# Attention with keys and values made beside it: the product with the values moved between two pieces of keys and values

## The reference

```python
q = (x @ Wq + bq).reshape(B, N, H, hd).transpose(0, 2, 1, 3)
kv = (ctx @ Wkv + bkv).reshape(B, K, 2, H, hd).transpose(2, 0, 3, 1, 4)
k, v = (kv[0], kv[1])
attn = jnp.einsum('bhnd,bhkd->bhnk', q * SCALE, k)
attn = jax.nn.softmax(attn, axis=-1)
out = jnp.einsum('bhnk,bhkd->bhnd', attn, v)
```

## Time and profile before

| | |
|---|---|
| median of 3 runs | 1428.68 us (1428.05 to 1432.59) |
| the profiled execution | 1433.56 us, its span 1431.5 us |
| PE busy | 1331.0 us, 93% |
| DVE, ACT, GpSimd busy | 937.2, 759.0, 101.6 us |
| DMA | 146.15 MB, mean 102 GB/s |
| mean granted TensorE clock | 0.974 |
| the batch loop (seven passes) | 81.80 to 880.86 us of the span |

### The profile page before, as it was taken

How to read it: one execution, slowest core, us unless ns; L and a number is a source line. 1 busy time by engine, 2 the same in 40 slices (tenths; PEclk the granted TensorE clock), 3 DMA queues, 4 the chain that set the end, 5 groups by cost and what they waited for, 6 DMA issues and landing times.

```text
span 1431.5 us, 21997 instructions
## 1 busy us (share of the span) xinstructions
PE 1331.0 (93%) x7407; PEld 1151.9 (80%) x7408; DVE 937.2 (65%) x1498; ACT 759.0 (53%) x1320; POOL 101.6 (7%) x75
## 2 busy tenths in 40 slices
PE   5999999999999999999999999956898799999995
PEld 4888888899889889888898889845777577878774
DVE  3666666667567666666666666648489836578772
ACT  3455565566556555555555555533332526578770
POOL 0000000000000000000000000063243120000001
PEclk9999999999999999999999999977899899999997
DMA  5121011110101112112101110570548357399983
GB/s 191 55 71 49 27 44 44 33 44 22 52 19 50 29 33 59 29 29 60 33 26 44 44 33 16 105 176 16 106 122 305 130 198 257 133 338 343 341 284 96
DMA packets 129443, 146.15 MB, mean 102 GB/s; under 512 B 66408, under 2 KB 69864, under 8 KB 129392
## 3 DMA queue, kind: packets, MB, share of 16 engines
q1 hardware_dynamic: 128128, 141.49, 32.1%
q0 software_dynamic: 1280, 4.20, 0.9%
HBM read 125.02 MB, written 20.12 MB: 101 GB/s over the span
## 4 chain that ended last, share of the span: by engine, by line
PE 70%; DVE 14%; issue 6%; DMA 5%; ACT 4%; SPq 1%; DVEq 0%; POOL 0%; ACTq 0%; POOLq 0%
PE ps_scores L151 12%; PE ps_scores L153 12%; PE ps_scores L152 12%; PE ps_out L779 6%; PE ps_turn L767 5%; PE ps_scores L756 5%; PE ps_turn L665 2%; DVE stat L621 2%; PE ps_scores L2009 2%; PE ps_scores L2007 2%; PE ps_scores L2008 2%; DMA wu_raw<-in_L_ffn_W_dram 2%; DMA b1rows<-b_parts 2%; DVE Ks L531 2%; DVE wu_lo L1903 1%
## 5 line engine op out<-in xcount | busy, mean ns | idle before, releaser
L531 DVE SCALAR_TENSOR_TENSOR Ks<-ps_scores,bkc,Ks 64x384 fp32r<-64x384 f32 (+2 forms) x254 | 160.5, 632 | 147.9 <-ACT Ks L415 144.8
L151 PE MATMUL ps_scores<-cT_hi,Wkv_hi 128*128 128x384 f32 (+2 forms) x508 | 184.6, 363 | 6.4 <-DVE Wkv_lo L553 6.4
L493 ACT ACTIVATE Pr<-ps_scores,stat 128x705 f32<-128x705 f32 (+1 forms) x128 | 119.6, 934 | 115.5 <-DVE stat L621 115.5
L153 PE MATMUL ps_scores<-cT_hi,Wkv_lo 128*128 128x384 f32 (+2 forms) x508 | 175.4, 345 | 0.0
L152 PE MATMUL ps_scores<-cT_lo,Wkv_hi 128*128 128x384 f32 (+2 forms) x508 | 175.0, 344 | 0.0
L415 ACT ACTIVATE Ks<-ps_scores,bkc 64x384 fp32r<-64x384 f32 (+2 forms) x254 | 149.6, 589 | 43.0 <-PE ps_scores L153 41.2
L151 PE MATMUL ps_scores<-Wkv_hi,cT_hi 128*128 128x512 f32 (+1 forms) x412 | 170.6, 414 | 0.5 <-DVE Ks L531 0.5
L480 ACT CAST PT<-ps_turn 128x512 fp32r<-128x512 f32 (+2 forms) x256 | 110.2, 483 | 110.4 <-PE ps_turn L767 109.6
L537 DVE TENSOR_TENSOR Vs<-ps_scores,Vs 128x512 fp32r<-128x512 f32 (+1 forms) x103 | 71.2, 691 | 148.9 <-ACT Vs L419 148.3
L153 PE MATMUL ps_scores<-Wkv_hi,cT_lo 128*128 128x512 f32 (+1 forms) x412 | 162.4, 394 | 0.0
L152 PE MATMUL ps_scores<-Wkv_lo,cT_hi 128*128 128x512 f32 (+1 forms) x412 | 161.8, 393 | 0.0
(11 more groups left out here) (355 smaller groups left out, 2455.0 us busy)
## 6 DMA issues: line engine op xcount, KB each, us to landing
wu_raw<-in_L_ffn_W_dram SPq DMA_DIRECT2D x64, 1024.0 KB, 7.5
raw<-in_ctx_dram SPq DMA_DIRECT2D x16, 768.0 KB, 4.6
raw<-in_ctx_dram SPq DMA_DIRECT2D x8, 1024.0 KB, 5.3
raw<-in_ctx_dram SPq DMA_DIRECT2D x8, 512.0 KB
sorted_x<-zeros SPq DMA_DIRECT2D x1, 4096.0 KB, 15.1
sorted_out<-zeros SPq DMA_DIRECT2D x1, 4096.0 KB, 25.6
o_heads<-U SPq DMA_DIRECT2D x56, 64.0 KB, 1.7
oA<-o_heads SPq DMA_DIRECT2D x8, 448.0 KB, 9.4
```

What stands on the lines that cost most here:

```text
L151: nc.tensor.matmul(out_ap, sh, mh, start=(i == 0), stop=False)
L153: last = nc.tensor.matmul(out_ap, sl, mh, start=False, stop=(i == len(pairs) - 1))
L493: nc.scalar.activation(Pr[:, i % 2, 0:VALID[c]], S_cols(c, 0, VALID[c]), ACT.Exp, bias=stat[:, 0, c, i:i + 1], accum_out=stat[:, 1, c, i:i ...
L531: ins = nc.vector.scalar_tensor_tensor(out=Ks[c][64:128, j, o:o + wide], in0=acc[64 * h:64 * h + 64, 0:wide], scalar=bkc[:, j:j + 1], in1= ...
```

## The change

In every step that makes pieces, outputs(i) on the tensor engine and the sum into U on the vector engine are issued behind the step's first piece (and the context turn behind it) and ahead of its second piece. Where a step has one piece the order stays what it was, except that work beside the unit now comes behind the outputs on PE in the last batch. In the last unit, which has no pieces, nothing changes. ACT's queue is the same.

```diff
--- before.py
+++ after.py
@@ -615,6 +615,13 @@
                                                           f32(PT[0:TAIL, tiles[-1], 0, :]), ALU.subtract)
                         ins.then_inc(sem("turn_lo"), 1)
 
+                    def sum_outputs(i):
+                        dve.wait_ge(sem("o_made"), pair0 + i)
+                        if i == 1:
+                            dve.wait_ge(sem("u_free"), b * 128 + (128 if beside else 64) * c + 1)
+                        nc.vector.tensor_reduce(U[:, i - 1, :], psO_heads.rearrange("p (a r) -> p r a", a=2),
+                                                AX.X, ALU.add).then_inc(sem("o_summed"), 1)
+
                     for i in range(STEPS):
                         if i < NP:
                             dve.wait_ge(sem("s_made"), pair0 + i + 1)
@@ -629,12 +636,10 @@
                                 if n == first[i] and i < ctx:
                                     cc, s = (1 - c, 1) if i < KC else (c, 0)
                                     ctx_lo(turn0 + turn_of_ctx(i), bank(C_BANK), cc, s, i % KC)
-                        if i >= 1:
-                            dve.wait_ge(sem("o_made"), pair0 + i)
-                            if i == 1:
-                                dve.wait_ge(sem("u_free"), b * 128 + (128 if beside else 64) * c + 1)
-                            nc.vector.tensor_reduce(U[:, i - 1, :], psO_heads.rearrange("p (a r) -> p r a", a=2),
-                                                    AX.X, ALU.add).then_inc(sem("o_summed"), 1)
+                                if n == first[i] and i >= 1:
+                                    sum_outputs(i)
+                        if i >= 1 and not ctx:
+                            sum_outputs(i)
                         if beside:
                             beside(i)
                     if c == 1 and not beside:
@@ -796,9 +801,11 @@
                                 if n == first[i] and i < ctx:
                                     bb, cc, s = (b + c, 1 - c, 1) if i < KC else (b + 1, c, 0)
                                     turn_ctx(turn0 + turn_of_ctx(i), bank(C_BANK), bb, cc, s, i % KC)
+                                if n == first[i] and i >= 1:
+                                    outputs(i)
                         if beside:
                             beside(i)
-                        if i >= 1:
+                        if i >= 1 and not ctx:
                             outputs(i)
 
                 with pe.Fori(0, BE) as b:
```

## The result

The changed kernel takes **1482.07 us** (median of four, 1480.34 to 1483.48) beside 1430.41 of the kernel before: a ratio of 1.0358 [1.0337, 1.0379], 52 us slower (a ratio is given with its 95% interval). Forecast were 1483.1 and a range of 1470 to 1494. The profiled execution took 1483.48, its span 1480.5 against 1431.5.

What follows compares the result with a forecast made beforehand. The tensor engine's in-order queue was taken as the bound. Waits of 3.08 and 3.30 plus 0.7 restart gave 7.1 us per batch, 49.7 for seven; with 4.7 for the last, +54.4: 1483.1 us, range 1470 to 1494.

Steps and rivals of the forecast that it cites:

- the restart: Tensor engine, outputs after a wait: the group spans 0.10 us more for each of seven new waits, 0.7 us per batch.
- The chain and its price: End of piece b to outputs: 4.88 us, without U (0.34) and a context-copy delay (0.23); cover 3.94, so 0.94 us wait.
- step 1: Outputs wait for the probabilities' low parts, per batch: 0.89 us in chunk 0, 0.91 in chunk 1.
- step 2: Outputs behind a step ending with keys wait, per batch: 0.94 us in chunk 0, 0.75 in chunk 1.
- step 5: Outputs wait 0.94 us per batch in each chunk; chunk 0's follows keys 322 wide.
- step 6: One-piece step, its old wait grows: chunk 0 to 0.95 us (+0.31; other count 1.12), chunk 1 to 0.93 (+0.38).
- piece 5: Chunk 1, first piece of step 3: new wait of 0.32 us per batch for the bank of piece 4.
- Steps 3, 4, 7 and 8: Chunk 0, behind values or a single piece whose outputs still follow it: no wait.
- The last pass: Last batch's chunk 0, outside the loop: 4.7 us more together; its chunk 1, without pieces, untouched.
- The faster case: Rival: only the one-piece step's wait changes as U leaves the chain, 8 or 10 us gained, 1420 us; 3 in 100.
- Absorbed in part: Rival: only first-step waits are real, later ones find the vector engine ahead; 16 us more, 1445 us; 5 in 100.
- The clock: Rival: tensor engine idling drops the loop's granted clock to 0.92, costing 69 us more, 1552 us; 2 in 100.

Runs made afterwards that it cites:

- The first run: The changed kernel with the vector engine's sum into U back behind both pieces, only the tensor engine's outputs moved: 1495.3 us, 1.0438 of the kernel before.
- the run with the steps behind values: The kernel before with outputs and sum moved only in steps 4 and 7 of chunk 0 and 3, 4 and 7 of chunk 1: 1436.15 us, 1.0027.
- the late low parts: The changed kernel, vector engine taking most last pieces' low parts behind the next maximum and probabilities' low parts, step 0's context copy behind the maximum: 1423.83 us, 0.9946.

## Why the prediction was right, step by step

- **The number, and the luck in it.** The forecast 1483.1 lies 1.0 from the median, but the growth was forecast as 54.4 and is 51.7; the forecast started from 1428.68, which came out as 1430.41 with a fourth run, and that hides 1.7. In the two profiled spans the growth is 49.0: of the 5.4 that are missing, 4.0 are the loop's (49.7 forecast, 45.7 measured), the restart below, and 1.4 the stretch ahead of the loop.
- **The chain and its price.** Forecast 4.88 us from the end of piece b, measured 4.89. Both things that were to fall out of it did: U stands at 454.11, ahead of the low parts, and those stand behind no context copy. The first run shows U's share by putting it back.
- **The waits, step by step** (forecast, then measured). Chunk 0: step 1 0.89, 0.89; step 2 0.94, 0.96; step 5 0.94, 0.95; step 6 0.95, 0.95. Chunk 1: 0.91, 0.91; 0.75, 0.79; piece 5 0.32, 0.34; 0.94, 0.95; 0.93, 0.95. Steps 3, 4, 7 and 8 wait in neither. For step 6 of chunk 0 two counts stood against each other, 1.12 and 0.94; the second, chain less cover, was right. Taking from and adding to the old wait misses that in the kernel before the low parts stood 0.19 behind a context copy there (462.80 against 462.58 + 0.03), which the later end of piece b takes out. In chunk 1 no copy stood in the way, and the same count gave 0.93 for a measured 0.95. What the new waits add sums to 3.10 + 3.39 = 6.49 a batch, 0.11 above the forecast 6.38 without the restarts.
- **The restart was the term mis-sized**: 0.7 us a batch were forecast, about 0.05 are there (6.54 less 6.49), and this is the forecast's excess of half a microsecond a batch. The outputs do take 0.93 from start to start (451.31 to 452.24) instead of 0.82. But they take as much where they don't wait, as the last section shows, and the piece that now follows them instead of a context turn is shorter by nearly the same: 452.24 to 454.35 is 2.11, where 432.30 to 434.47 was 2.17; 322 wide it is 1.78 for 1.86, 512 wide 2.75 for 2.84. The step that failed is the reading of a longer group behind a wait as the price of the wait, from the two groups that waited, without a look at one behind a context turn that didn't.
- **The two halves of a rule.** The Trainium skill (TensorE: Matmul & The Clock Gate, "Part 2: What happens when you issue a matmul") says that weight loads are pulled ahead of matmuls in flight and that matmuls keep their order. From the first half the prediction drew a rival, a restart that costs nothing. It nearly is so, but not by weights that were loaded ahead over the wait: the loads waited with their products (PEld rows for L609 and L613, 52.5 us in all). The second half the trace shows at each wait: piece b starts at 460.18, behind the outputs of 459.24.
- **The last pass.** Forecast +4.7; from its first scores to the end of the program 4.7 were measured, 4.5 of them in chunk 0's unit itself (54.25 to 58.78). Step 1 waits 1.38 (1.32 forecast), step 5 1.29 (0.94 + 0.35), step 6 grew by 0.48 for 0.31, step 3 by 0.25 where 0.5 was estimated. The terms are right to 0.25, and the agreement of the sum is closer than that of its terms.
- **The rivals.** The faster case needed the low parts of step 1 to end before the outputs could start; they end 0.89 after, as read. "Absorbed in part" fell with step 2's wait; its move alone costs 10 us in the loop (1.45 a batch). The clock stayed at 1.00 through the loop with 5% of it empty in waits of up to 0.97 us. The Trainium skill's section "A second HAM failure mode: psum-queue depth-cycling" on the same page tells of another kernel whose short idles between groups of matmuls made the clock swing; the gaps of this loop did not do it.
- **A sign that failed.** Busy time was to stay near 1331 us; it is 1340.1, drawn longer as told above. The other signs came: waits of 39.6 us in the named steps, 0.34 at piece 5, the wait before the scores of step 1 as it was.
- **What the prediction did not say.** A wait can be bought two steps away: step 4's move delays the chain of step 5, as the run with the steps behind values showed, and its sentence "steps 3, 4, 7, 8: no wait" is true without being "no cost". In the full change it does not come on top: there step 5's outputs wait as well, so step 6's wait is set by chain and cover from the end of step 5 (0.95 forecast and measured).
- **Why the change costs** is thus shown from both ends: the tensor engine's order alone gives all of the loss, and the same order with the chain cut at its first link (the late low parts) gives none of it.

## What to carry to other kernels

In a queue that runs in order, an operation's place decides which wait the work in front of it covers: count the chain of what it waits for from its own start event, and the work that the queue has left in between, before and after the move. Where two engines drain a bank, the place of the consumer and the moment of the second drain belong to one decision: here the moved outputs alone cost 52 us, the late drain alone 27, and both together gain 8, or 12 with the copy early and piece 2's drain early again. And count on to the next steps: a piece that now ends right where a chain starts delays that chain, even where nobody waits for it yet.

## What the runs showed of the hardware that was not expected

The first group of products behind transposes takes about 0.08 to 0.1 us longer from start to start, be it outputs, a piece of any width or scores (0.92 for 0.82), and whether it waits or not. In the kernel before, a step with one piece shows it without a wait:

```profile
447.22 0.44 PE L665 MATMUL ps_turn<-ident,raw 128*128 128x128 f32 x3
447.46 1.07 PE L779 MATMUL ps_out<-PT,Vs 128*128 128x256 f32 x7
448.37 0.58 PE L756 MATMUL ps_scores<-Ks,Qs_hi 128*128 128x448 f32 x2
```

0.91 us, and 0.82 for the same seven behind a piece (434.47 to 435.29). In step 8 of chunk 0 of the changed kernel, behind a piece as well:

```profile
500.64 0.98 PE L784 MATMUL ps_out<-PT,Vs 128*128 128x256 f32 x7
501.47 0.49 PE L761 MATMUL ps_scores<-Ks,Qs_hi 128*128 128x354 f32 x2
```

0.83. Behind a wait it was 0.93 (451.31 to 452.24), so the wait itself adds 0.02 at most. What in the engine takes the time was not tried. The excess goes to whichever group comes next behind the transposes, and so an exchange of places behind the same transposes neither costs nor saves it.
